# Keys and values projected for two groups at once in a fused attention kernel

## What is computed

```python
x = x + tanh(g_xattn[0]) * autocorrelation(layernorm(x), ctx, ctx)
x = x + tanh(g_ffn[0]) * routed_lora_ffn(layernorm(x))
# third layer, hidden = layernorm(x):
q = (hidden @ Wq.T)   # 32 heads of 128
k = (ctx @ Wk.T)      # 8 heads of 128
v = (ctx @ Wv.T)      # 8 heads of 128
q = _rmsnorm(q, q_norm_w)
k = repeat(k, 4); v = repeat(v, 4)
k = _rmsnorm(k, k_norm_w)
scores = einsum('bhqd,bhkd->bhqk', q, k) / sqrt(128) + mask
probs = softmax(scores)
out = einsum('bhqk,bhkd->bhqd', probs, v)
x = x + tanh(g_xattn[1]) * (out @ Wo.T)
x = x + tanh(g_ffn[1]) * lora_ffn(layernorm(x))
```

## Time and profile before

| | |
|---|---|
| median of 3 runs | 715.75 us (715.5 to 719.91) |
| the profiled execution | 715.24 us |
| its span, first to last instruction | 713.4 us |
| TensorE busy | 702.8 us, 99% |
| VectorE, ScalarE, GpSimdE busy | 569.2, 378.9, 373.6 us |
| granted TensorE clock | 1.00 of full speed (2.4 GHz) |

### The profile page before, as it was taken

How to read it: one execution, slowest core, us unless ns; L and a number is a source line. 1 busy time by engine, 2 the same in 40 slices (tenths; PEclk the granted TensorE clock), 3 DMA queues, 4 the chain that set the end, 5 groups by cost and what they waited for, 6 DMA issues and landing times.

```text
span 713.4 us, 12679 instructions
## 1 busy us (share of the span) xinstructions
PE 702.8 (99%) x3690; PEld 571.5 (80%) x3690; DVE 569.2 (80%) x1171; ACT 378.9 (53%) x1094; POOL 373.6 (52%) x431
## 2 busy tenths in 40 slices
PE   8899999999999999999999999999999999999998
PEld 5565556687888888888888888888888888888876
DVE  4899997667878877887888778778877887778985
ACT  4577765456456545544564546445555554455430
POOL 1568876647545534643464257344634563247533
PEclk9999999999999999999999999999999999999999
DMA  9311104145776775676566666766675667545431
GB/s 324 127 31 45 45 15 162 39 122 141 230 225 168 209 194 135 187 206 175 158 189 193 174 170 168 217 155 174 165 214 155 170 182 209 138 123 155 123 100 74
DMA packets 109283, 110.31 MB, mean 155 GB/s; under 512 B 12576, under 2 KB 78240, under 8 KB 108960
## 3 DMA queue, kind: packets, MB, share of 16 engines
q1 hardware_dynamic: 109216, 109.51, 54.4%
HBM read 69.62 MB, written 39.85 MB: 153 GB/s over the span
## 4 chain that ended last, share of the span: by engine, by line
PE 70%; issue 8%; POOL 8%; DVE 7%; DMA 3%; ACT 2%; SPq 1%; DVEq 0%; POOLq 0%; ACTq 0%
PE pair L1075 17%; PE pair L1076 17%; PE pair L1077 17%; PE pair L1175 6%; PE pair L1121 3%; POOL qkr L648 3%; DVE qkn L1597 2%; DMA pTf<-p_scratch 1%; POOL wo_lo L635 1%; POOL prob L640 1%; SPq L487 1%; PE pair L1138 1%; PE pair L1104 1%; PE pair L1105 1%; PE pair L1155 1%
## 5 line engine op out<-in xcount | busy, mean ns | idle before, releaser
L877 ACT ACTIVATE prob<-score,nmax 128x128 f32<-128x128 f32 x256 | 99.8, 391 | 132.2 <-DVE nmax L1562 131.7
L640 POOL TENSOR_TENSOR prob<-prob,erec 128x512 f32<-128x512 f32 x64 | 66.7, 1041 | 111.1 <-DVE erec L1582 111.1
L1075 PE MATMUL pair<-wo_hi,oT_hi 128*128 128x512 f32 x256 | 106.4, 415 | 0.2 <-issue 0.2
L1075 PE MATMUL pair<-wq_hi,nT_hi 128*128 128x512 f32 x256 | 101.3, 396 | 0.0
L1076 PE MATMUL pair<-wo_lo,oT_hi 128*128 128x512 f32 x256 | 100.0, 391 | 0.0
L1077 PE MATMUL pair<-wo_hi,oT_lo 128*128 128x512 f32 x256 | 99.9, 390 | 0.0
L1077 PE MATMUL pair<-wq_hi,nT_lo 128*128 128x512 f32 x256 | 99.7, 389 | 0.0
L1076 PE MATMUL pair<-wq_lo,nT_hi 128*128 128x512 f32 x256 | 99.7, 389 | 0.0
L1587 DVE TENSOR_REDUCE qkss<-qksq 128x5 f32<-128x640 f32 x64 | 52.3, 818 | 53.2 <-ACT qksq L884 52.8
L884 ACT ACTIVATE qksq<-pair 128x640 f32<-128x640 f32 x64 | 44.9, 702 | 74.2 <-PE pair L1077 74.0
L648 POOL TENSOR_TENSOR qkr<-qkse,neghalf 128x5 f32<-128x5 f32 x64 | 76.6, 1196 | 5.4
(11 more groups left out here) (176 smaller groups left out, 1693.9 us busy)
## 6 DMA issues: line engine op xcount, KB each, us to landing
qk_scratch<-qk_blocks SPq DMA_DIRECT2D x256, 80.0 KB, 1.9
qkT<-qk_scratch SPq DMA_DIRECT2D x64, 320.0 KB, 3.0
p_scratch<-p_blocks SPq DMA_DIRECT2D x256, 64.0 KB, 1.8
pTf<-p_scratch SPq DMA_DIRECT2D x64, 256.0 KB, 3.3
wq_raw<-in_wq SPq DMA_DIRECT2D x32, 256.0 KB, 4.0
wo_raw<-in_wo SPq DMA_DIRECT2D x32, 256.0 KB, 4.5
wkv_raw<-in_wkv SPq DMA_DIRECT2D x8, 512.0 KB, 5.2
ctxn<-in_ctx_n SPq DMA_DIRECT2D x8, 256.0 KB, 3.3
```

Source lines behind the costliest of these rows:

```text
L640: pool.tensor_tensor(prob[:], prob[:], erec[:].unsqueeze(2).broadcast_to([P, BL, P]), ALU.mult).then_inc(normed, 1)
L877: t = act.activation(prob[:, i, :], score[:, i, :], ACT.Exp, bias=nmax[:, i:i + 1], accum_out=esum[:, i:i + 1])
L1075: pe.matmul(out, l_hi, r_hi, start=start, stop=False)
```

## The change

Groups are taken in pairs. In the slots of an even group `project_kv` multiplies 512 columns, the keys and the values of both groups of the pair (the weights are laid out as keys of both, values of both); in the slots of an odd group it is not called. So a slot whose projection is for an even group has 12 passes of 512 columns in place of 12 of 256, and one for an odd group has none.

The keys and values of the odd group have to be kept for eight slots: in an even slot six heads are squared and summed, the odd key is scaled into `odd_k`, the odd value is split into `odd_v_hi` and `odd_v_lo`. In an odd slot four heads are squared, summed, scaled and turned, the key's blocks are turned from `odd_k` by an instruction of its own, and nothing is split for values.

These take room. The raw query weights land in the place of the low half that they become (`under` gives one place to two tiles), so do the raw key and value weights, and key and value weights are held once. A load therefore waits until the projections of the group that used the place are done (`load_wkv`, `load_wq`). Key and value weights come in four chunks of 256 KB per pair; `WKV_LOAD` and `WQ_LOAD` give the slots of their loads, `WKV_AT` the slots (of 16) in which they are split, 8, 9, 12 and 13. Output weights are split two in slot 2 of a group and two in slot 3, before one and three. The query chunks keep their slots; where a key and value chunk stands in the same slot, GpSimdE subtracts the query chunk behind `inverse_norms` in place of ahead of it. The fourth layer's weights land elsewhere (`w1`, `lA`, `lBc`, `y`), those of `w1` in two halves.

The diff, cut:

```diff
-    WKV_AT, WO_AT = 0, 3
+    WO_AT = 3
     WQ_AT = {1: (0,), 2: (1,), 4: (2,), 5: (3,)}
-    FIRST_WKV_LOAD = 7
+    WQ_LOAD = {-1: (0, 1), 0: (2, 3)}
+    WKV_LOAD = {6: (0, 1), 7: (2, 3)}
+    WKV_AT = {8: (0,), 9: (1,), 12: (2,), 13: (3,)}
...
+        def under(name, shape):
+            with ExitStack() as place:
+                return place.enter_context(nc.sbuf_tensor(name, shape, F32))
...
+        wq_raw1 = under("wq_raw1", [P, CH, D])
+        wq_lo1 = sb("wq_lo1", [P, CH, D], F32R)
...
         def kv_bank(n):
-            return pair[buf(n)][:, HG * P:(HG + 2) * P]
+            return bank[2 * buf(n) + 1]
+        def even(n):
+            return n // B % 2 == 0
+        def heads(n):
+            return HG + 2 if even(n) else HG
...
+                def load_wkv(p, c):
+                    sp.wait_ge(qkv_done, B * (2 * p - 1))
+                    sp.dma_start(wkv_raw[:, c, :], wkv_d[p][:, c, :]).then_inc(ld_wkv[c], 16)
...
                 def slot(n):
                     g = n // B
                     norm_probs(n - 1)
-                    if wkv_at(n):
-                        low_wkv(g + 1)
-                    for c in wq_at(n):
-                        low_wq(g + 1, c)
+                    low_wkv(g // 2 + 1, wkv_at(n))
+                    if not wkv_at(n):
+                        for c in wq_at(n):
+                            low_wq(g + 1, c)
                     if n > B and n % B == WO_AT:
-                        for h in range(1, HG):
+                        for h in range(2, HG):
                             low_wo(g, h)
                     inverse_norms(n + 2)
+                    if wkv_at(n):
+                        for c in wq_at(n):
+                            low_wq(g + 1, c)
                     if n > B and n % B == WO_AT - 1:
                         low_wo(g, 0)
+                        low_wo(g, 1)
...
                 def high_v(n):
+                    if not even(n):
+                        return
...
-                    act.activation(v_hi[:, n % RING, :], v_bank(n), ACT.Copy).then_inc(v_h, 1)
+                    act.activation(v_hi[:, n % RING, :], v_bank(n, 0), ACT.Copy)
+                    act.activation(odd_v_hi[:, odd_at(n), :], v_bank(n, 1), ACT.Copy).then_inc(v_h, 1)
...
                 def project_qkv(n):
-                    project_q(n, range(CH))
-                    project_kv(n).then_inc(qkv_done, 1)
+                    t = project_q(n, range(CH))
+                    if even(n):
+                        t = project_kv(n)
+                    t.then_inc(qkv_done, 1)
...
                 def scale_qk(n):
...
+                    if even(n):
+                        t = dve.tensor_scalar(odd_k[:, odd_at(n), :], qk_bank(n, h, h + 1)[:, 0, :],
+                                              qkr[:, h:h + 1], None, ALU.mult)
...
-        "wkv": np.concatenate([wk, wv], axis=3).reshape(G, P, CH * 2 * P),
+        "wkv": np.concatenate([wk[0::2], wk[1::2], wv[0::2], wv[1::2]], axis=3),
```

More of the change, by code:

```diff
@@ L233, in kv_bank, with qk_bank, v_bank, v_count @@
         def kv_bank(n):
-            return pair[buf(n)][:, HG * P:(HG + 2) * P]
-        def qk_bank(n):
-            return pair[buf(n)][:, 0:(HG + 1) * P].rearrange("p (h t) -> p h t", h=HG + 1)
-        def v_bank(n):
-            return pair[buf(n)][:, (HG + 1) * P:(HG + 2) * P]
+            return bank[2 * buf(n) + 1]
[3 more added lines that the diff above has]
+            return HG + 2 if even(n) else HG
+        def qk_bank(n, first, last):
+            return pair[buf(n)][:, first * P:last * P].rearrange("p (h t) -> p h t", h=last - first)
+        def v_bank(n, odd):
+            return pair[buf(n)][:, (HG + 2 + odd) * P:(HG + 3 + odd) * P]
+        def v_count(n):
+            return n // (2 * B) * B + min(n % (2 * B), B)
+        def odd_at(n):
+            return (n + B // 2) % B
         def queries(n, i):
@@ L310, in flamingo_kernel @@
         ld_wo = [sem(f"c_wo_loaded{h}") for h in range(HG)]
-        ld_wkv = sem("c_wkv_loaded")
+        ld_wkv = [sem(f"c_wkv_loaded{c}") for c in range(CH)]
         ld_mask = sem("c_mask_loaded")
@@ L405, in wkv_at @@
         def wkv_at(n):
-            return on(n) and on(n + B) and n == (3 if n < B else n // B * B + WKV_AT)
+            return WKV_AT.get(n % (2 * B), ()) if on(n) and on(n + 2 * B) else ()
         def wq_at(n):
@@ L507, in read_probs @@
                     sp.dma_start(pTf[:], p_dram[n % 2].rearrange("j z h r -> (j z) (h r)")).then_inc(p_in[n % 2], 16)
-                load_wkv(1)
-                for c in range(CH):
-                    load_wq(1, c)
                 sp.wait_ge(w_fwd, 2 * B)
@@ L525, in _ @@
                         read_probs(n - 1)
+                    if n in (2, 3):
+                        for c in (2 * n - 4, 2 * n - 3):
+                            load_wq(1, c)
+                    k = (n + 1) // B
+                    if n > 0 and 1 <= k < G - 1:
+                        for c in WQ_LOAD.get(n - k * B, ()):
+                            load_wq(k + 1, c)
                     if n > 0 and g + 2 < G:
-                        if n == FIRST_WKV_LOAD if n < B else wkv_at(n - 1):
-                            load_wkv(g + 2)
-                        for c in wq_at(n - 1):
-                            load_wq(g + 2, c)
+                        for c in WKV_LOAD.get(n % (2 * B), ()):
+                            load_wkv(g // 2 + 1, c)
                     if n > 0 and g + 1 < G and b == WO_AT + 1:
@@ L989, in slot @@
                         high_wo(g, 0)
+                        high_wo(g, 1)
                     exponents(n)
@@ L1179, in project_q @@
                 def project_q(n, chunks):
-                    g, even, here = n // B, n // B % 2, at(n)
+                    g, here = n // B, at(n)
                     need(pe, qk_nat, last_in_buf(n))
@@ L1603, in turn_qk @@
                         dve.wait_ge(qk_out[(n - 1) % 2], BL * landed(n - 1))
[L1604 to L1605 removed]
+                    blocks = qk_blocks[:].rearrange("p (j h y) -> p h j y", j=BL, h=HG + 1)
+                    h = HG + 1 if even(n) else HG
+                    t = dve.transpose(blocks[:, 0:h], qkn[:, 0:h].rearrange("p h (j z) -> p h j z", j=BL))
+                    if not even(n):
+                        t = dve.transpose(blocks[:, HG], odd_k[:, odd_at(n), :].rearrange("p (j z) -> p j z", j=BL))
+                    t.then_inc(qk_turned, 1)
                 def add_batch(b):
```

154 lines of the change are left out of this document (79 added, 75 removed).

## The result

The changed kernel takes 734.1 us (median of 4 runs, 733.0 to 734.7) against 716.2 of the kernel before (median of 4): a ratio of 1.0239, 95% interval 1.022 to 1.0258. The forecast was 715.2, and its range ended at 724.

The account below looks back on a forecast made before the run. TensorE's matmuls were taken to bound each slot while chains returning to it have slack. 715.24 - 4.5 - 0.7 + 3.2 + 1.5 + 0.5 = 715.2 us; own range 712 to 719, 8 in 10 for 709.5 to 724.

Parts of the forecast that it names:

- Term 3: Short slots with weight loads and conversions: lateness stops TensorE 1.05 us per pair of groups, three pairs; +3.2 us (0 to 9).
- the tightest loop: Probabilities' exchange across two short slots: exponents can start after 13.63 us against 14.06, slack 0.4 us.
- the stop forecast for slot 11: Two output chunks ahead of the keys on ScalarE leave 0.7 of 1.7 us slack; TensorE stops 0.3 us.
- That for slot 13: Lateness of 2.45 us from slot 12, 0.75 above the slack, stops TensorE in slot 13.
- Term 1: TensorE's key and value passes: 64 slots at 1.43 us become 32 at 2.72 us; -4.5 us.
- Term 2: Start: extra matmuls cover the first slots' waits for the exchange of queries and keys; -0.7 us (-1.3 to +0.5).
- VectorE's loop: VectorE's work in a short slot takes 6.54 us against 7.03, so it fits with 0.5 us to spare.
- Term 5: Quiet short slots: the 0.4 us slack hides the median transfer landing but not its tail; +0.5 us (0 to 9).
- Term 4: Tail: VectorE, also doing second-stage statistics, is late in the last group's short slots and TensorE stops; +1.5 us (0 to 4).
- The slower one: Exchange of probabilities sets the short slots, deciding above a mean landing of 3.7 us; 724.2 us, chance 0.19.
- Wider passes cost more: Double-width projection passes cost more than two single ones; 238 ns would take the gain, 719.7 us; chance 0.04.
- No term for single-buffered places: Weights in the low halves' places cost nothing themselves, though loads wait for the group using the place; no term.

Follow-up runs that it names:

- queries_first: Changed kernel with, in slot 13, the last query-weight chunk converted ahead of the last key and value chunk; 733.1 us.
- no_conversions: Changed kernel with all loads, without converting key and value weights for the second to fourth pair and query weights for groups 3, 5 and 7; 732.6 us.
- own_queue: Changed kernel with its loads of key and value weights and of query weights for groups 3, 5 and 7 issued by ScalarE on its own queue; 737.8 us.
- no_loads_no_conversions: Changed kernel without loads and conversions of key and value weights for the second to fourth pair and query weights for groups 3, 5 and 7; 720.7 us.
- padded: Changed kernel with two more TensorE passes of 512 columns in each of the 32 odd slots, output unchanged; 735.3 us.
- spread_loads: Changed kernel with the same weight loads spread, 256 KB per turn (512 KB in the last), and odd groups' wo two turns later; 728.1 us.

## Why the prediction was wrong

- **The step that failed** is the price of a load in Term 3, and with it the claim that the exchange of probabilities is the tightest loop, with a slack of 0.4. A load beside the exchange was priced at 0.6 us on the read of the probabilities and at nothing on the writes of queries and keys. I had given that chain 1.8 us of slack and no lateness at all: it was in the list of slacks and in no sum. Loads delay those writes by 1.9 us in the landing and 2.3 from write to read. The stop of 2.11 us at 366.27 can be added up. In the quiet slot the writes start 1.26 us before the scores (341.04 and 342.30), here 0.11 before (356.75 and 356.86): 1.15 late, of which 0.89 is SyncE issuing four loads. To the read it is 2.29 longer. From the read to the next scores it is 3.40 in place of 4.48, 1.08 of slack used up. 1.15 + 2.29 - 1.08 = 2.36, by which that interval is longer than 7.05. This is read from the trace; no run delayed those writes alone.
- **The read of the probabilities** was late too, by more than 0.6. With the 512 KB behind it, it landed after 5.1 us (issued at 205.64) and 4.6 (at 346.14), against a median of 3.3 before. So the predicted chain, in which ScalarE is late with the keys, did stop TensorE, for 2.0 us in three waits. One of them is the stop forecast for slot 11, with two output chunks ahead of its keys: 0.8 us at 520.68, for 0.3. In the first pair that slot's scores waited 0.6 us (at 240.72), but there the keys were waiting for their transfer, and in the second not at all. That for slot 13 had another cause: with two conversions in it the low half of the last query chunk came late for the projection, 1.7 us in three waits, and interval 13 was 2.9 us over its quiet length in the three pairs. That "the last chunk is converted in slot 13, before slot 14 uses it" and needs no term was wrong.
- **Term 3 (+3.2, at most 9)** measured 16.4 us, of which the runs give the loads 7.0 to 11.9 and the conversions 1.6 to 6.5, by whether the other is there (13.5 together, over the whole kernel; the wo weights and what wasn't taken apart have the rest). The 0.6 us for a read with a load behind it was taken from the earlier trace rows, where a slot of 8.46 us gave transfers time to recover; the 1 MB was weighed by its landing and not by what it does to the writes that follow it.
- **Term 1 (-4.5)** and **Term 2 (-0.7)** came to -2.8 together. The start was right: 9.5 us behind at slot 5, where eight wide projections cost 10.3; that is some 1.5 of the 2.8. The rest is the size of Term 1: a pass of 512 columns took 231 ns in place of 227, so a long slot 9.84 in place of 9.75, and each pair of slots wins 0.04 us in place of 0.14, 1.3 us for 32 pairs. The rule of the Trainium skill (TensorE: Matmul & The Clock Gate, Back-to-back issue gap), which I set aside with its 1.0 us, was nearer than my 4.5. Its 109 and 216 ns are not what the rows show, but that doubling the columns nearly doubles the time was right.
- **VectorE's loop** fits, as read: quiet short slots run at 7.05 us with TensorE busy throughout, as forecast (7.03), and **Term 5 (+0.5)** for quiet slots was not needed. Slots 53 and 54 run at 7.05 too. So the exchange fits a short slot when nothing stands beside it.
- **Term 4 (+1.5, at most 4)** measured 5.0. Of it 1.65 us are in interval 55, beside the loads of w1, lA and lB, for which I had no term. 1.7 lie in the folding slots 56 to 60, as expected, and 1.7 in interval 61, where the scores wait for the keys and these for the transfer of queries and keys.
- **The rivals.** The slower one (724.2) named the right kind of case, no slack in short slots, and a transfer that has a part in it but not the larger one. It was to decide at a mean landing of the probabilities above 3.7 us; their median over the stage was 3.1, and 4.2 only beside the loads (345 to 370 us), where TensorE's one long stop was for queries and keys. Wider passes cost more, the third, was half true (231 of the 238 ns).
- **A clock that falls behind a stop** stood in no term: 1.7 us, after the longest stop.
- **No term for single-buffered places** holds for the loads: none waited for its place longer than 0.4 us. But the place of the low halves is what forces all loads between slots 5 and 12, all of them short. That was the cost of the shared place, and I didn't price it.

## What to carry to other kernels

When a change makes slots uneven, check each chain against the shortest slot, with the loads and conversions that will stand in that slot, and let none out of the sum because its slack is positive in a quiet one. A transfer's landing time is not a constant of the kernel: ask what a load does to the small writes that come after it, on whatever queue. A wait that ends last tells who was late, not who made it late: the run that took away the last wait (queries_first) won nothing that can be told from the noise, the one that made all slots equally long won everything back.

## What the runs showed of the hardware

- Writes of 80 KB with a median landing of 1.8 us (320 to 345 us, with 1 MB of loads well ahead of them) took 3.7 in a stretch with 2 MB of loads close to them (345 to 370), and 3.6 when the loads were issued on another engine's queue.
- A stop of TensorE of 2.1 us was followed by a slot at a granted clock of 0.81, one of 3.2 us in no_conversions by one at 0.80 (1.7 us longer each). Other runs have more such pairs: 2.75 us in own_queue and 1.94 in queries_first, followed by 0.80 and 0.81; 1.88 us in no_loads_no_conversions by 0.82; 1.84 in queries_first and 1.73 in padded by 1.00. In spread_loads, where interval 26 stopped for 0.6 us, the next ran at 1.00.
- A matmul of 512 columns in this stream takes 229 to 231 ns beside the exchange, and took 227 before; one of 256 columns took 119.
